# Cross-attention in a decoder layer: where a step's projection tiles stand in TensorE's program

## The chip, the cores and the metric

One core of a Trainium2 chip runs the whole program. The metric is device time in microseconds: the median of three runs. A profile of one execution gives the busy times and the waits.

## The reference

The reference is one decoder layer on x of shape (8, 128, 512), in float32: self-attention with 32 heads, cross-attention with a context of the same shape, a feed-forward part, and a layer norm after each. The change is in the cross-attention, which computes:

```
q = (x @ wq)  -> 32 heads of 128      k, v = (ctx @ wk), (ctx @ wv) -> 8 heads of 128
q, k = rope(q), rope(k)               each k and v head serves 4 query heads
attn = softmax(q @ k.T / sqrt(128) + mask)
out  = (attn @ v, heads side by side) @ wo
```

## The kernel before

**Number format.** Each operand of a product is held as a high and a low half, and each product is made of three matmuls (high by high, low by high, high by low; `product`, line 30). So every copy from PSUM has two parts: ScalarE writes the high half, and VectorE or POOL (GpSimd) the low half, as the difference.

**Steps.** `attend_cross` (line 623) goes over 8 groups g of four query heads that share one k and v head, and in each group over the 8 batch rows s. That makes 64 steps, n = 8g + s, with three more at the end to drain. Groups 1 to 6 are a hardware loop. In step n the core computes the scores of row n, transposes the probabilities of n-2, multiplies them by v, and multiplies the result of n-3 by wo.

**Projections.** While a group is attended, the next one is projected, half of the rows at a time. A half cycle is four steps; u = s % 4 is the place in it. It projects six tiles of 128 by 512, each with 12 matmuls: four query heads (tiles 0 to 3), k (tile 4) and v (tile 5). The places do tiles 0 and 1, tile 2, tiles 3 and 4, tile 5 (`STEPS`, line 631). Even tiles use one PSUM bank, odd ones another. Tiles 0 to 4 are then rotated: three operations on VectorE (`rotate`, line 952), a sum on POOL (line 1060), the high half on ScalarE (line 774), the low half on POOL (line 1065). Tile 5 is copied by ScalarE (line 780) and transposed on TensorE (`turn_values`, line 881).

**Order.** Each engine runs its own program in order, one `step` after another, and semaphores tie them together. The orders are written by hand:

- TensorE (line 888): transposes of the probabilities of n-2 (line 896), scores of n (lines 906, 907), in place 0 the transposes of v, the output product of n-3 with wo (`yb`), the probability-value product of n-2 (`ov`), then the step's projection tiles (`project`, line 863).
- VectorE (line 967): reciprocal, low half of the transposes, mask added to the scores, four maxima, their negation (line 997), in place 0 the low half of v, the output product added to x (line 1007), the low half of `ov` (line 1010), in row 2 the low halves of two pieces of wo (line 1015), then the rotations of this step's tiles.
- ScalarE (line 794): copy of the transposes, high halves of the tiles projected in the step before, four exponentials (line 817), copy of `ov` (line 792), high halves of weight pieces (line 828), in place 3 the copy of tile 5.
- POOL (line 1068): probabilities of n-1 divided by their sums (line 1075), low halves of the tiles of the step before, low halves of weight pieces (line 1088), sums of the rotations of this step.
- SP loads the weight pieces into a ring of five slots, each as the split of the piece before it in that slot ends.

**What a tile waits for.** `project` waits for both halves of its weight piece and for its PSUM bank. For tiles 2 to 5 the bank is free when VectorE has rotated the tile two before (`s_sin`); for tile 0 the rotations of the half cycle before must be done; tile 1 waits for ScalarE's copy of the last tile 5 (`s_vt`). VectorE rotates the tiles of a step as the last work of that step (in the last group, a row's statistics follow).

Of the kernel before, what the change touches and what calls it, by code (L numbers as in the profile page):

```python
# [12 lines left out]
B = 8  # L13
# [16 lines left out]
def product(eng, out, stationary, moving, first, last):  # L30


    for n, (i, j) in enumerate(PASSES):
        mm = eng.matmul(out, stationary[i], moving[j], start=first and n == 0,  # L34
                        stop=last and n == len(PASSES) - 1)
    return mm
# [156 lines left out]
def wait(eng, sem, value):  # L193

    if not isinstance(value, int) or value > 0:
        eng.wait_ge(sem, value)
# [426 lines left out]
def attend_cross(nc, first, wq_d, wk_d, wv_d, wo_d, mask_d, trig_d, ident, xT, cT, w, stage, y, norm, next_norm, weights):  # L623
# [7 lines left out]
    STEPS = {0: (0, 1), 1: (2,), 2: (3, 4), 3: (5,)}  # L631
    K, V, TILES = 4, 5, 6
    PER = 10
    with ExitStack() as ctx:
# [25 lines left out]
        s_chi, s_clo = sem("chi"), sem("clo")  # L660
# [5 lines left out]
        NX = 2 * C  # L666
# [5 lines left out]
        def live(g, s, lag=0):  # L672
            return not isinstance(g, int) or 0 <= B * g + s - lag < NS

        def loop(eng, step):


            for s in range(B):
                step(0, s)
            with eng.Fori(1, G - 1) as g:  # L680
                for s in range(B):
                    step(g, s)
            for g in (G - 1, G):
                for s in range(B):
                    step(g, s)

        def projects(g, s):
            return not isinstance(g, int) or g < G - 1 or (g == G - 1 and s < 4)

        def half_cycle(g, s):  # L690

            return 2 * g + 1 + s // 4
# [7 lines left out]
        def lo_of(g, j):  # L700

            return TILES * g + j + 1
# [22 lines left out]
        @block.sync  # L725
        def _(eng):
            eng.dma_start(trig[:, :, :], trig_d).then_inc(s_const, 16)
            eng.dma_start(mask[:, :, :], mask_d).then_inc(s_const, 16)

            def wait_first(n):  # L730
                kind, j = first.PIECES[n]
                eng.wait_ge(s_wlo if kind == "w" else s_clo, j + 1)

            for n in range(RING, FIRST):
                wait_first(n - RING)
                first.load(eng, n)

            def cycle(g, last=False):
                for j in range(Q if last else PER):
                    what = ("wo", j) if j < Q else ("w", j - Q)  # L740

                    if j < RING and isinstance(g, int) and g == 0:
                        wait_first(FIRST + j - RING)
                    elif j < RING:
                        eng.wait_ge(s_wlo, lo_of(g, j + 1))
                    elif j < PER - 1:
                        h = j - RING
                        eng.wait_ge(s_wolo[h // 2], 2 * g + h % 2 + 1)
                    else:
                        eng.wait_ge(s_wlo, lo_of(g + 1, 0))  # L750
                    src = wo_d[bass.ds(g, 1), :, j, :] if j < Q else \
                        wq_d[bass.ds(g + 1, 1), :, j - Q, :] if j < Q + K else (wk_d if j == Q + K else wv_d)[bass.ds(g + 1, 1)]
                    eng.dma_start(stage[:, slot(what), :], src.rearrange("a p n -> (a p) n")).then_inc(s_piece[slot(what)], 16)

            cycle(0)
            with eng.Fori(1, G - 1) as g:
                cycle(g)
            cycle(G - 1, last=True)
            eng.wait_ge(s_wlo, TILES * G)
            for i in range(2):  # L760
                eng.wait_ge(s_wolo[i], 2 * G)
            for n in range(len(weights.PIECES)):
                weights.load(eng, n)
# [97 lines left out]
        @block.tensor  # L861
        def _(eng):
            def project(H, g, half, j):

                i = TILES * H + j
                eng.wait_ge(s_whi, PER * g + j + 1)
                eng.wait_ge(s_wlo, lo_of(g, j))

                if j == 0:
                    wait(eng, s_sin, 5 * H)  # L870
                elif j == 1:
                    wait(eng, s_vt, H)
                else:
                    eng.wait_ge(s_sin, 5 * H + j - 1)
                cols = slice(half * HALF, (half + 1) * HALF)
                for c in range(C):
                    mm = product(eng, pj[j % 2][:, :], [t[:, j, c * P:(c + 1) * P] for t in w],
                                 [t[:, c, cols] for t in (xT if j < K else cT)], c == 0, c == C - 1)
                mm.then_inc(s_pj, 1)

            def turn_values(H):
                eng.wait_ge(s_vt, H + 1)
                wait(eng, s_vlo, H)
                for t in range(4):
                    mm = eng.transpose(vp[:, t * P:(t + 1) * P], vt[:, t * S:(t + 1) * S], ident)
                mm.then_inc(s_vp, 1)

            def step(g, s):
                n = B * g + s
                H = half_cycle(g, s)  # L890
                u, half = s % 4, 1 - s // 4
                if live(g, s, 2):
                    eng.wait_ge(s_norm, n - 1)
                    wait(eng, s_plo, n - 2)
                    for h in range(Q):
                        mm = eng.transpose(tp[:, h * S:(h + 1) * S], prob[:, s % 2, h * S:(h + 1) * S], ident)  # L896
                    mm.then_inc(s_tp, 1)
                if live(g, s):
                    if u == 0:
                        eng.wait_ge(s_qlo, 5 * H)  # L900
                    wait(eng, s_top, n)
                    tok = slice(s * S, (s + 1) * S)
                    for h in range(Q):
                        out = sc[:, h // 2, h % 2, :, :].rearrange("p j s -> p (j s)")
                        both = k[:, s, :, :].rearrange("p j s -> p (j s)")
                        eng.matmul(out, q[0][:, h, tok], both, start=True, stop=False)  # L906
                        mm = eng.matmul(out[:, 0:S], q[1][:, h, tok], both[:, 0:S], start=False, stop=True)
                    mm.then_inc(s_sc, 1)
                if isinstance(g, int) and g == 0 and s == 0:
                    eng.wait_ge(norm.s_lo, B)  # L910
                    eng.wait_ge(s_clo, NX)
                if u == 0 and live(g, s):
                    turn_values(H - 1)
                if live(g, s, 3):
                    m = n - 3
                    eng.wait_ge(s_ohi, m + 1)
                    eng.wait_ge(s_olo, m + 1)
                    wait(eng, s_add, m)
                    if s == 3:
                        for i in range(2):  # L920
                            eng.wait_ge(s_wolo[i], 2 * (g + 1))
                    for h in range(Q):
                        mm = product(eng, yb[:, :], [t[:, h * S:(h + 1) * S] for t in o],
                                     [t[:, h, :] for t in wo], h == 0, h == Q - 1)
                    mm.then_inc(s_y, 1)
                if live(g, s, 2):
                    m = n - 2
                    eng.wait_ge(s_phi, m + 1)
                    eng.wait_ge(s_plo, m + 1)
                    wait(eng, s_olo, m)  # L930
                    if u == 2:
                        eng.wait_ge(s_vlo, 2 * g + 1 + s // 4)
                    mm = product(eng, ov[:, :], [t[:, (s - 2) % B, :] for t in v], [t[:, :] for t in pT], True, True)
                    mm.then_inc(s_pv, 1)
                if projects(g, s):
                    for j in STEPS[u]:
                        project(H, g + s // 4, half, j)

            for b in range(4):
                norm.transpose(eng, b)  # L940
            eng.wait_ge(norm.s_lo, 4)
            for j in range(TILES):
                if j == K:
                    eng.wait_ge(s_clo, C)
                project(0, 0, 0, j)
            for b in range(4, B):
                norm.transpose(eng, b)
            loop(eng, step)

        @block.vector  # L950
# [556 lines left out]
```

## Time and profile before

| | us |
|---|---|
| median of three runs | 1065.37 (1063.99 to 1065.83) |
| span of the profiled execution | 1065.3 |
| TensorE busy | 987.9 (93%) |
| VectorE busy | 765.2 (72%) |
| ScalarE busy | 503.1 (47%) |
| POOL busy | 437.0 (41%) |

The page gives no time around the span; the span and the median differ by less than 0.1 us. A share of the span is a mean over stages: self-attention comes first, the cross-attention's steps run from about 312 to 926 us, and the feed-forward part ends the program. Busy times of TensorE are modelled from starts, so its work is better read from the distance of one start to the next.

### The profile page before, as it was taken

The numbers are of one execution on the slowest core, as the hardware profiler recorded it, in microseconds if no ns is written. First come the engines' busy times: TensorE is split into PE (matmuls) and PEld (weight loads), VectorE is DVE, ScalarE is ACT, GpSimd is POOL, SyncE is SP. The second block draws the span as 40 slices with busy tenths as digits, with TensorE's granted clock in tenths as the row PEclk, the third lists the DMA queues.
The fourth block names the chain that finished last, engine by engine and source line by source line (L and its number), as shares of the span: only waits on it lengthen the run. The fifth ranks groups of instructions, "written<-read, shape, count | busy, mean of one in ns | idle before, by whom it ended". The sixth has DMA issues, their size and how long they took to land. (4 is left out here: it accounts for less than half of the span.)

```text
span 1065.3 us, 17470 instructions
## 1 busy us (share of the span) xinstructions
PE 987.9 (93%) x4940; PEld 825.1 (77%) x4940; DVE 765.2 (72%) x2345; ACT 503.1 (47%) x1581; POOL 437.0 (41%) x367
## 2 busy tenths in 40 slices
PE   6997999999778999999999999999999999789996
PEld 5875999999556887887887887787778777578885
DVE  4445568888697787777877877777777788784646
ACT  4325669898335435445345435444444435441220
POOL 1762000000357556546546646637546455340101
PEclk9997579999899999999999999999999999999998
DMA  8032212222221102002002002002001002210001
GB/s 298 1 99 60 60 37 59 46 58 70 87 82 50 40 11 65 31 5 69 30 0 76 22 0 79 20 0 79 20 15 64 10 18 73 78 62 10 30 1 39
DMA packets 41372, 52.02 MB, mean 49 GB/s; under 512 B 5104, under 2 KB 21616, under 8 KB 41200
## 3 DMA queue, kind: packets, MB, share of 16 engines
q1 hardware_dynamic: 41008, 50.44, 15.6%
q0 software_dynamic: 320, 1.05, 0.3%
q8 instruction: 21, 0.34, 0.1%
q14 instruction: 23, 0.19, 0.1%
HBM read 40.98 MB, written 2.10 MB: 40 GB/s over the span
## 5 line engine op out<-in xcount | busy, mean ns | idle before, releaser
L1060 POOL TENSOR_TENSOR C_t<-C_t 128x512 f32<-128x512 f32 x80 | 104.5, 1310 | 153.2 <-DVE C_t L965 153.2
L817 ACT ACTIVATE C_prob<-C_prob,C_ntop 128x128 f32<-128x128 f32 x256 | 99.8, 391 | 87.9 <-DVE C_ntop L997 87.8
L34 PE MATMUL C_yb<-C_woh,C_oh 128*128 128x512 f32 x256 | 107.5, 420 | 17.4 <-POOL C_wol L1088 12.3
L774 ACT ACTIVATE C_qh<-C_t 128x512 fp32r<-128x512 f32 x64 | 40.5, 633 | 141.0 <-POOL C_t L1060 141.0
L1010 DVE TENSOR_TENSOR C_ol<-C_ov,C_oh 128x512 fp32r<-128x512 f32 x64 | 44.2, 691 | 85.8 <-ACT C_oh L792 85.8
L34 PE MATMUL C_pj<-xTh,wh 128*128 128x512 f32 x256 | 101.3, 396 | 3.7 <-DVE xTl L128 2.2
L492 ACT ACTIVATE B_prob<-B_prob,B_ntop 128x128 f32<-128x128 f32 x256 | 99.2, 392 | 8.5 <-DVE B_ntop L573 7.3
L34 PE MATMUL C_yb<-C_woh,C_ol 128*128 128x512 f32 x256 | 102.8, 402 | 0.0
L34 PE MATMUL C_yb<-C_wol,C_oh 128*128 128x512 f32 x256 | 102.6, 401 | 0.0
L34 PE MATMUL C_pj<-xTh,wl 128*128 128x512 f32 x256 | 100.8, 394 | 0.0
L34 PE MATMUL C_pj<-xTl,wh 128*128 128x512 f32 x256 | 100.6, 393 | 0.0
L1065 POOL TENSOR_TENSOR C_ql<-C_t,C_qh 128x512 fp32r<-128x512 f32 x64 | 82.3, 1297 | 3.0 <-ACT C_qh L774 3.0
L961 DVE TENSOR_TENSOR C_t<-C_pj,C_trig 128x512 f32<-128x512 f32 x80 | 55.0, 687 | 32.7 <-PE C_pj L34 30.9
L1088 POOL TENSOR_TENSOR wl<-stage,wh 128x512 fp32r<-128x512 f32 x42 | 53.8, 1288 | 55.8 <-ACT wh L828 55.8
L34 PE MATMUL B_sc<-kd,qs 128*128 128x512 f32 x192 | 69.8, 479 | 5.7 <-PEq L226 3.1
L801 ACT ACTIVATE C_pTh<-C_tp 128x512 fp32r<-128x512 f32 x64 | 37.5, 586 | 76.0 <-PE C_tp L896 76.0
L1075 POOL TENSOR_TENSOR C_prob<-C_prob,C_rden 128x512 f32<-128x512 f32 x64 | 66.7, 1042 | 15.7 <-DVE C_rden L974 15.7
L34 PEld LDWEIGHTS C_yb<-C_woh,C_oh 128*128 128x128 f32 x256 | 49.5, 193 | 29.6 <-issue 17.7
L906 PE MATMUL C_sc<-C_k,C_qh 128*128 128x256 f32 x256 | 67.8, 342 | 2.1 <-POOL C_k L1065 2.1
L527 PE MATMUL B_ov<-vhl,B_pTl 128*128 (+1 forms) x256 | 66.0, 278 | 0.0
L596 DVE TENSOR_TENSOR B_pTl<-B_tp,B_pTh 128x512 fp32r<-128x512 f32 x64 | 44.1, 689 | 30.2 <-ACT B_pTh L485 30.2
L101 POOL TENSOR_TENSOR first_norm_rstd<-first_norm_moments,power 128x4 f32<-128x4 f32 x2 | 2.1, 1032 | 148.8 <-DVE first_norm_moments L88 148.8
(219 smaller groups left out, 2867.1 us busy)
## 6 DMA issues: line engine op xcount, KB each, us to landing
stage<-wq_dram SPq DMA_DIRECT2D x32, 256.0 KB, 3.4
stage<-wo_dram SPq DMA_DIRECT2D x32, 256.0 KB, 3.1
qs<-q SPq DMA_DIRECT2D x16, 256.0 KB, 2.7
kd<-k SPq DMA_DIRECT2D x128, 32.0 KB, 2.0
stage<-wqkvT_dram SPq DMA_DIRECT2D x10, 256.0 KB, 5.9
x<-x_nat_dram SPq DMA_DIRECT2D x1, 2048.0 KB, 10.1
stage<-wk_dram SPq DMA_DIRECT2D x8, 256.0 KB, 3.2
stage<-ctxT_dram SPq DMA_DIRECT2D x8, 256.0 KB, 3.0
```

The source lines that it names most:

```text
L34: mm = eng.matmul(out, stationary[i], moving[j], start=first and n == 0, stop=last and n == len(PASSES) - 1)
L492: last = eng.activation(e, e, ACT.Exp, bias=ntop[:, G % 4, h:h + 1], scale=1.0, accum_out=total[:, HG * G + h:HG * G + h + 1])
L527: mm = eng.matmul(out[:, at:at + DH], pT[1][:, G % 2, h * S:(h + 1) * S], v[:, 0:DH], start=False, stop=True)
L596: eng.tensor_tensor(pT[1][:, G % 2, :], tp[G % 2][:, :], pT[0][:, G % 2, :].bitcast(F32), ALU.subtract).then_inc(s_plo, 1)
L817: last = eng.activation(e, e, ACT.Exp, bias=ntop[:, s % 2, h:h + 1], scale=1.0, accum_out=total[:, s % 2, h:h + 1])
L906: eng.matmul(out, q[0][:, h, tok], both, start=True, stop=False)
L961: eng.tensor_tensor(split(t1[:, j % 2, :]), split(bank[:, :]), cos, ALU.mult).then_inc(s_cos, 1)
L1010: eng.tensor_tensor(o[1][:, :], ov[:, :], o[0][:, :].bitcast(F32), ALU.subtract).then_inc(s_olo, 1)
L1060: eng.tensor_tensor(t1[:, j % 2, :], t1[:, j % 2, :], t2[:, j % 2, :], ALU.add).then_inc(s_sum, 1)
L1065: eng.tensor_tensor(lo, t1[:, j % 2, :].rearrange("p (b s) -> p b s", s=S), hi.bitcast(F32), ALU.subtract).then_inc(s_qlo, 1)
L1075: eng.tensor_tensor(e, e, rden[:, (s - 1) % 2, :].unsqueeze(2).broadcast_to([P, Q, S]), ALU.mult).then_inc(s_norm, 1)
L1088: eng.tensor_tensor(lo, stage[:, slot(what), :], hi.bitcast(F32), ALU.subtract).then_inc(s_wolo[1] if kind == "wo" else s_wlo, 1)
```

## The change

In TensorE's `step`, the projection tiles move from the end of the step to its start, ahead of the transposes. The two waits of step 0 for the transposed x and the context move with them. Nothing else changes: no other engine's program, no semaphore, no buffer.

```
@@ def step(g, s), TensorE
                 u, half = s % 4, 1 - s // 4
+                if isinstance(g, int) and g == 0 and s == 0:
+                    eng.wait_ge(norm.s_lo, B)
+                    eng.wait_ge(s_clo, NX)
+                if projects(g, s):
+                    for j in STEPS[u]:
+                        project(H, g + s // 4, half, j)
                 if live(g, s, 2):
                     eng.wait_ge(s_norm, n - 1)
...
                     mm.then_inc(s_sc, 1)
-                if isinstance(g, int) and g == 0 and s == 0:
-                    eng.wait_ge(norm.s_lo, B)
-                    eng.wait_ge(s_clo, NX)
                 if u == 0 and live(g, s):
                     turn_values(H - 1)
...
                     mm.then_inc(s_pv, 1)
-                if projects(g, s):
-                    for j in STEPS[u]:
-                        project(H, g + s // 4, half, j)
```

## Rows read from the trace of the kernel before

**Rows 1.** Windows of the cross-attention: bounds, length, busy us (count) per engine, PEclk, DMA.
```profile
311.67:344.66 32.99, 28.51 (x138) 23.45 (x138) 25.51 (x77) 16.07 (x50) 19.48 (x16) 0.95 0.13 40
344.66:882.92 538.26, 519.60 (x2577) 430.36 (x2577) 413.77 (x1134) 242.19 (x725) 304.28 (x251) 0.99 0.10 34
```

**Rows 2.** Timeline, TensorE, steps 0 and 29: start us, us, operation, idle before and releaser.
```profile
313.01 0.66 PE L885 MATMUL C_vp<-ident,C_t 128*128 128x128 f32 x4 [0.21 <-DVE xTl L128]
313.43 0.48 PE L34 MATMUL C_pj<-xTh,wh 128*128 128x512 f32 x1
...
585.93 0.60 PE L896 MATMUL C_tp<-ident,C_prob 128*128 128x128 f32 x4
...
587.24 0.45 PE L34 MATMUL C_yb<-C_woh,C_oh 128*128 128x512 f32 x1
```

**Rows 3.** Timeline, TensorE, the rest of step 29 and the start of 30.
```profile
590.05 0.39 PE L34 MATMUL C_ov<-C_pTh,C_vh 128*128 128x512 f32 x1
...
590.74 0.39 PE L34 MATMUL C_pj<-xTh,wh 128*128 128x512 f32 x1
...
593.46 0.60 PE L896 MATMUL C_tp<-ident,C_prob 128*128 128x128 f32 x4
```

**Rows 4.** Waits, TensorE, 282 to 890: us in total, times, longest.
```profile
PE C_yb L34 <- POOL C_wol L1088: 12.3, 8, 1.8
...
PE C_pj L34 <- DVE C_t L965: 4.9, 3, 2.0
```

**Rows 5.** Timeline, ScalarE, step 29 and the start of 30.
```profile
586.57 0.60 ACT L801 ACTIVATE C_pTh<-C_tp 128x512 fp32r<-128x512 f32 x1 [4.34 <-PE C_tp L896]
587.08 0.64 ACT L774 ACTIVATE C_qh<-C_t 128x512 fp32r<-128x512 f32 x1
...
592.08 0.40 ACT L817 ACTIVATE C_prob<-C_prob,C_ntop 128x128 f32<-128x128 f32 x1 [1.65 <-DVE C_ntop L997]
...
593.64 0.58 ACT L792 ACTIVATE C_oh<-C_ov 128x512 fp32r<-128x512 f32 x1
594.12 0.62 ACT L828 ACTIVATE wh<-stage 128x512 fp32r<-128x512 f32 x1
```

**Rows 6.** Timeline, VectorE, steps 28 and 30.
```profile
579.37 0.17 DVE L997 TENSOR_SCALAR C_ntop<-C_top 128x4 f32<-128x4 f32 x1
...
597.09 0.66 DVE L977 TENSOR_TENSOR C_pTl<-C_tp,C_pTh 128x512 fp32r<-128x512 f32 x1
...
599.41 1.26 DVE L997 TENSOR_SCALAR C_ntop<-C_top 128x4 f32<-128x4 f32 x1
...
602.88 0.69 DVE L1010 TENSOR_TENSOR C_ol<-C_ov,C_oh 128x512 fp32r<-128x512 f32 x1 [1.61 <-ACT C_oh L792]
603.48 0.68 DVE L961 TENSOR_TENSOR C_t<-C_pj,C_trig 128x512 f32<-128x512 f32 x1
...
605.62 0.69 DVE L961 TENSOR_TENSOR C_t<-C_pj,C_trig 128x512 f32<-128x512 f32 x1
```

**Rows 7.** Timeline ahead of the loop: end of a rotation on VectorE, start on TensorE.
```profile
293.07 0.68 DVE L965 TENSOR_TENSOR C_t<-C_pj,C_trig 64x512 f32<-64x512 f32 x1
293.90 0.47 PE L34 MATMUL C_pj<-xTh,wh 128*128 128x512 f32 x1 [1.45 <-DVE C_t L965]
```

**Rows 8.** Timeline, POOL, step 30.
```profile
599.36 1.29 POOL L1065 TENSOR_TENSOR C_ql<-C_t,C_qh 128x512 fp32r<-128x512 f32 x1
```

**Rows 9.** Timeline, VectorE, step 2: its two splits of wo.
```profile
333.68 1.28 DVE L1015 TENSOR_TENSOR C_wol<-stage,C_woh 128x512 fp32r<-128x512 f32 x2
```

**Rows 10.** Timeline, TensorE, one stall ahead of step 2's probability-value product.
```profile
328.09 0.76 PE L34 MATMUL C_ov<-C_pTh,C_vh 128*128 128x512 f32 x1 [2.76 <-issue]
```

**Rows 11.** Windows after two stalls and around a third, with the granted clock.
```profile
328.09:331.21 3.12, 3.12 (x7) 2.45 (x8) 2.71 (x12) 0.93 (x2) 2.76 (x3) 0.50 0.00 0
...
412.40:418.00 5.60, 3.87 (x17) 3.25 (x18) 5.44 (x17) 1.24 (x3) 5.60 (x6) 1.00 0.79 231
...
491.80:495.17 3.37, 3.37 (x9) 2.60 (x8) 3.26 (x15) 1.26 (x2) 3.37 (x4) 0.50 0.54 181
```

## The prediction

> **What bounds the kernel now.** I read the page first, then the stretches, then the waits of TensorE, then one step on each engine. The chain that ended last covers only the tail of the program and says nothing of the cross-attention, so the stretch table decides. From the score products of step 4 to those of step 60 it shows 538.26 us, with TensorE busy 519.60 of them at clock 0.99; VectorE comes next with 413.77 [rows 1]. That stretch is 14 half cycles of four steps, 38.45 us each. TensorE's own work in one half cycle, from starts to next starts [rows 2, 3]: six projection tiles of 2.72 (590.74 to 593.46), four times transposes and scores 1.31 (585.93 to 587.24), output product 2.81 (to 590.05) and probability-value product 0.69 (to 590.74), one value transpose 0.42 (313.01 to 313.43): 16.3 + 19.2 + 0.4 = 36.0. So 2.5 us of a half cycle are lost now. The one wait that recurs is the output product on POOL's split of wo, 12.3 us in 8 waits; projection tiles wait for a rotation on VectorE three times only, 4.9 us, and all three lie ahead of the loop [rows 4]. The tiles at a step's end are what keeps TensorE busy while ScalarE and VectorE finish that step.
>
> **What the change does.** Per tile it moves 12 matmuls, their 12 weight loads and their semaphore waits, from behind the probability-value product to ahead of the transposes. No instruction is added or removed and no DMA belongs to a tile. Nothing moves on SP, POOL, ScalarE or VectorE; the two waits moved in step 0 are for work that ends where the trace starts the value transposes. SP's weight loads hang on splits that wait for a tile's end, which comes no later within a step than now; at no cost.
>
> The cost is in what a tile waits for. Tile 2 (place 1) needs the rotation of tile 0, tile 4 (place 2) that of tile 2, tile 5 (place 3) that of tile 3: each time a rotation that VectorE issues as the last thing of the step before, behind its max, its add of the output product and its split of the probability-value product. Today a tile comes a step's worth of TensorE work after that; then it stands first. Queued behind the waiting tile on TensorE are the transposes and scores of that very step, from which ScalarE and VectorE live, so nobody can work ahead.
>
> **The path in one step.** From the first transpose to the next tile: copy of the transposes starts after 0.64 and takes 0.60 [rows 2, 5]; VectorE's low half, mask add and four maxima take 2.32 up to the negation [rows 6]; negation 0.17; four exponentials 1.56; copy of the probability-value product 0.58 [rows 5]; its split 0.60, the rotation's three operations 2.11 (2.14 to the next rotation's start) [rows 6]; TensorE starts 0.15 after a rotation ends (293.07 + 0.68 to 293.90) [rows 7]. With three or four hand-overs at 0.03 to 0.04 that is 8.87.
>
> The negation took 0.17 or 1.26. The long one begins at 599.41 and ends at 600.67, with POOL's split that ran from 599.36 to 600.65 [rows 6, 8]: it waits out the POOL operation. In place 1 POOL then splits two tiles behind the copies, starting 1.8, 3.05 after the transposes (0.64, 0.51 to the next ScalarE start, 0.64 [rows 5], then 1.29 each [rows 8]); the negation is due at 3.6, inside the second, which ends at 4.3. I take 0.55 there; bounds 0 and 1.1. In place 2 only one such split is left and it is over by 3.1.
>
> **The sum of a half cycle.**
> - Place 0: two tiles, 5.44; transposes and scores 1.31, values 0.42, output 2.81, probability-value 0.69, its drain 0.16 (0.39 long, 0.23 apart); then copy, split, rotation and hand-overs 3.50: 14.33. TensorE is idle 3.5 of it.
> - Place 1: 2.72 + 8.87 + 0.55 = 12.1. TensorE reaches tile 3 after 7.53 (2.72 + 1.31 + 2.81 + 0.69) and is through it after 10.25: idle about 1.8 before tile 4.
> - Place 2: 2.72 + 8.87 = 11.6, TensorE idle 3.9. Once in two half cycles VectorE also splits two pieces of wo here: 1.28 [rows 9].
> - Place 3: 7.53; the next two tiles need nothing that is late. Only in the half cycles with wo the second of them waits for ScalarE's two weight copies (0.52 each [rows 5]) and its value copy ahead: 0.8.
>
> Together 45.6, and for two half cycles 91.2 + 1.3 + 0.8 = 93.3 against 76.9 now (538.26 / 7): 8.2 more per half cycle, with the 1.7 us wait on wo gone (POOL has a step longer for it) and counted in the 76.9. Over 14: 115. The first half cycle now takes 32.99 [rows 1]; by the same path, with the products that its first steps lack left out, tile 0 starts near 313.0 [rows 2], tile 2 comes 11.2 after it, tile 4 8.3 later, tile 5 12.9 (8.87, 2.72 and wo's 1.28), the next tile 0 8.3 (7.53 and 0.8) and the scores of step 4 another 5.8: 359.5, where they stand at 344.66, 14.8 later. At step 60 there are no tiles to go ahead of the scores, so 5.4 comes off. Sum at full clock: 115 + 14.8 - 5.4 = 124.
>
> **The clock.** After the idle 2.76 us at 328.09 TensorE ran at half rate, 0.50 granted (1.2 of 2.4 GHz), seven matmuls in 3.12 us, 0.43 apart where 0.23 is usual; that is 1.4 lost, and 1.6 with an eighth [rows 10, 11]. Of the eight waits on wo, seven last about 1.7 us; three of the seven were followed by such a spell (491.80 to 495.17) and four not (412.40 to 418.00 stayed at 1.00) [rows 4, 10, 11]. So each of the two long stalls of a half cycle, 3.5 and 3.9, will bring one; as part of the spell can fall into the stall itself I take 1.2 of a possible 1.6 (bounds 0 and 1.6): 15 x 2 x 1.2 = 36. The 1.8 before tile 4 brings one three times in seven: 15 x 0.43 x 1.2 = 8. The tile that runs slow stands on the path, so this adds in full: 44.
>
> The Trainium skill, TensorE: Matmul & The Clock Gate, section "HAM oscillation — how this bites in real kernels", warns of just such a gap that returns in every turn of a loop, but sets the harm at gaps longer than those of 1.7 to 2.8 us after which the rows here show the fall; the trace disagrees on that point. [...]
>
> Forecast: 1065.3 + 124 + 44 = 1233. The span of the profiled execution, 1065.3, is within 0.1 of the median of the runs, 1065.37, so the sum stands against either.
>
> **Rivals.**
> 1. The stalls come but the clock stays, except after the longest (3.9 + 1.3, once a cycle): 1065.3 + 124 + 7 x 1.2 = 1198. For it: four of seven gaps of 1.7 left the clock at 1.00. Against: 2.76 did not. Chance 0.16. [...]
> 2. Only the stall at tile 2 bites, because VectorE, whose chain now runs beside the tiles, gets ahead by places 2 and 3: 36.0 + 3.7 + 0.8 a half cycle, 2.0 more than now, 30 in 15, and a spell of slow clock each, 18: 1114. For it: VectorE has 124 us of slack over the stretch. Against: it stands in order behind this step's scores. Chance 0.10.
> 3. The other side: TensorE gets faster. The wait on wo (1.7 in each of seven cycles) and its three slow spells go, 12 + 5, and tiles run on without waiting: 1048. It decides at tile 2: if VectorE's rotation of tile 0 is done when TensorE leaves place 0. It would have to be issued ahead of the split that needs the probability-value product, and in VectorE's program it is behind it. Chance 0.03; that no more than noise comes of all this, 0.02.
> 4. Everything is paid in full: 1.6 per spell, 1.1 at the negation, tile 4 slow each time: 124 + 15 x 0.55 + 15 x 3 x 1.6 = 204, 1270. Chance 0.07.
>
> **Numbers.** The forecast's own case has 0.62. Range 1188 to 1258: from no clock loss at all (1065 + 124) to most of the fourth case. About 0.2 is left outside, most of it below. A change under 0.2% (2 us) can't be told from none. Faster 0.03, same 0.02, slower 0.95.
>
> **What would show it.** In the profile after: TensorE idle ahead of the projection tiles for the rotation (its last line on VectorE), some 45 waits, 9 to 10 us per half cycle, and 130 to 150 in all where there are 4.9 now; the wait on POOL's split of wo gone or nearly; the eight steps of a cycle some 99 us apart instead of 77; TensorE's clock of the stretch at 0.90 to 0.94. ScalarE's and VectorE's busy times stay as they are, apart from the negation's. It would be wrong if a tile's wait ended on something else (the low half of a weight piece, for which POOL stands), if the transposes' wait on POOL's normalisation came last, or if a cycle came out under 90 us.

## The result and the profile after

The changed kernel takes 1248.42 us (median of four runs, 1245.05 to 1250.24) where the kernel before takes 1064.68 beside it (1062.39 to 1065.83). The ratio is 1.1739, with an interval of [1.1683, 1.1796]. The forecast was 1233, its range 1188 to 1258. The profiled execution has a span of 1247.5 us, 182.2 more than before.

First the stretches of the program after: bounds, length, busy time and count of PE, PEld, DVE, ACT and POOL, granted clock, DMA share, GB/s. The bounds are the score products of steps 0, 4 and 60 and the end.

```profile
318.59:364.87 46.28, 32.20 (x140) 25.68 (x138) 23.72 (x75) 16.28 (x50) 23.01 (x19) 0.82 0.11 38
364.87:1062.50 697.63, 558.49 (x2556) 452.20 (x2553) 395.29 (x1132) 237.37 (x719) 301.46 (x248) 0.91 0.08 26
1062.50:1247.50 185.00, 162.34 (x749) 131.78 (x747) 116.87 (x263) 58.73 (x137) 42.96 (x40) 0.95 0.11 38
```

Against [rows 1], the 14 half cycles from step 4 to step 60 take 159.4 us more (697.63 against 538.26). The scores of step 4 come 20.2 later (364.87 against 344.66), and from step 60 to the end it is 2.6 more (185.00 against 1065.30 - 882.92 = 182.38). TensorE's clock in the long stretch fell from 0.99 to 0.91, and it stood idle for 139 us of it (697.63 - 558.49) where it was 19.

The waits of TensorE from 300 to 1090 (us in all, times, longest) say for what:

```profile
PE C_pj L34 <- DVE C_t L965: 148.9, 46, 7.1
PE C_pj L34 <- POOL wl L1088: 5.7, 7, 0.8
```

The rotation on VectorE (line 965), three waits in [rows 4], now stops TensorE 46 times, 45 of them in the half cycles (the first, 2.0 us long, lies ahead of step 0, as before). The wait of the output product on wo is gone. One half cycle on TensorE's timeline, the first matmul of the tile after each stall (start, duration, operation, idle before and releaser); the first row is the same tile 5 in the half cycle before, where VectorE also splits wo:

```profile
549.48 0.79 PE L34 MATMUL C_pj<-cTh,wh 128*128 128x512 f32 x1 [5.01 <-DVE C_t L965]
...
574.90 0.51 PE L34 MATMUL C_pj<-xTh,wh 128*128 128x512 f32 x1 [3.43 <-DVE C_t L965]
...
588.73 0.50 PE L34 MATMUL C_pj<-cTh,wh 128*128 128x512 f32 x1 [1.70 <-DVE C_t L965]
...
600.34 0.79 PE L34 MATMUL C_pj<-cTh,wh 128*128 128x512 f32 x1 [3.82 <-DVE C_t L965]
```

Tile 2 waits 3.43, tile 4 1.70, tile 5 3.82 or 5.01: three stalls in each of the 15 half cycles. What the clock does behind them stands in windows that begin where these stalls end, that of tile 2 with its second matmul (columns as above):

```profile
549.48:556.09 6.61, 6.61 (x25) 5.34 (x25) 2.27 (x5) 0.68 (x2) 4.99 (x5) 0.60 0.47 154
575.24:578.62 3.38, 3.38 (x9) 2.61 (x8) 1.88 (x4) 0.00 (x0) 2.52 (x3) 0.50 0.22 70
588.73:593.00 4.27, 4.27 (x25) 3.72 (x26) 0.30 (x2) 0.77 (x2) 2.29 (x2) 1.00 0.19 61
```

Tile 5 starts at half rate (1.2 of 2.4 GHz), tile 2 too in this half cycle, tile 4 runs at full rate.

### The profile page after: what moved, and what is told of

Read it like the earlier page. It is cut to its first block and busy times, and to the rows that moved or that the text cites. A ratio compares the mean times of both kernels' runs of the same rounds, so it can differ in the third digit from the quotient of the medians.

```text
span 1247.5 us, 17458 instructions
## 1 busy us (share of the span) xinstructions
PE 1040.7 (83%) x4940; PEld 857.0 (69%) x4940; DVE 746.4 (60%) x2345; ACT 499.8 (40%) x1581; POOL 438.0 (35%) x367
## 3 DMA queue, kind: packets, MB, share of 16 engines
q0 software_dynamic: 320, 1.05, 0.3%
## 5 line engine op out<-in xcount | busy, mean ns | idle before, releaser
L977 DVE TENSOR_TENSOR C_pTl<-C_tp,C_pTh 128x512 fp32r<-128x512 f32 x64 | 44.1, 690 | 230.5 <-ACT C_pTh L801 230.5
L34 PE MATMUL C_pj<-xTh,wh 128*128 128x512 f32 x256 | 110.2, 430 | 64.2 <-DVE C_t L965 54.4
L34 PE MATMUL C_pj<-cTh,wh 128*128 128x512 f32 x128 | 67.9, 531 | 97.5 <-DVE C_t L965 97.5
L817 ACT ACTIVATE C_prob<-C_prob,C_ntop 128x128 f32<-128x128 f32 x256 | 99.8, 391 | 117.9 <-DVE C_ntop L997 117.8
L34 PEld LDWEIGHTS C_pj<-cTh,wh 128*128 128x128 f32 x128 | 32.2, 252 | 117.3 <-DVE C_t L965 83.2
L34 PEld LDWEIGHTS C_pj<-xTh,wh 128*128 128x128 f32 x256 | 53.1, 207 | 84.9 <-DVE C_t L965 46.6
L34 PE MATMUL C_pj<-xTh,wl 128*128 128x512 f32 x256 | 108.6, 424 | 0.0
L34 PE MATMUL C_pj<-xTl,wh 128*128 128x512 f32 x256 | 107.6, 420 | 0.0
L34 PE MATMUL C_pj<-cTl,wh 128*128 128x512 f32 x128 | 63.9, 499 | 0.0
```

Of the source, the lines that this page charges most:

```text
L817: last = eng.activation(e, e, ACT.Exp, bias=ntop[:, s % 2, h:h + 1], scale=1.0, accum_out=total[:, s % 2, h:h + 1])
L977: eng.tensor_tensor(pT[1][:, :], tp[:, :], pT[0][:, :].bitcast(F32), ALU.subtract).then_inc(s_plo, 1)
```

## The experiments

Each ratio is to the kernel before, on the same chip. "Excess" is the median less that kernel's own median there; the change's own is 183.7.

**1. A third PSUM bank for the tiles.** The bank of the value transposes joins the ring, so that a tile waits for a rotation one tile older.

```
+        def bank_of(H, j):
+            return pj[j % 2] if isinstance(H, int) and H == 0 else (*pj, vp)[j % 3]
...
+                elif j == 2:
+                    eng.wait_ge(s_vlo, H)
                 else:
-                    eng.wait_ge(s_sin, 5 * H + j - 1)
+                    eng.wait_ge(s_sin, 5 * H + j - 2)
```

> Tiles first as in the change, but over three PSUM banks (the value bank vp takes tiles 2 and 5), so that a tile waits for a rotation one step older. Theory W (the time is the wait of tiles 2, 4 and 5 for a rotation that VectorE issues last in the step before): the 152 us of waits on rotations fall below 10, the clock returns to 0.98 or more, and what is left is the wait on POOL's split of wo in row 3, longer than the 1.7 us of before since one tile instead of two lies ahead of it, some 4.4 us a cycle: 1070 to 1100 us. Rival O (the order itself: transposes and scores behind the tiles starve ScalarE and VectorE, the bank has no part in it): stays above 1220 us.

Measured: 1141.28 (1139.72 to 1142.84), ratio 1.0760 [1.0692, 1.0828], excess 81. TensorE's waits, 300 to 1000:

```profile
PE C_pj L34 <- POOL wl L1095: 24.2, 13, 3.2
PE C_yb L34 <- POOL C_wol L1095: 22.3, 8, 3.3
PE C_vp L34 <- POOL wl L1095: 18.0, 6, 3.0
...
PE C_pj L34 <- DVE C_t L972: 1.9, 1, 1.9
```

The rotation is gone from the list but for one wait, and with it 102 us of the excess: the dependency, not the order as such, makes the stalls. The time expected was missed on the high side, and the clock of the stretch comes back to 0.95 only, not to 0.98. In place of the rotation the low halves of weight pieces come last: of the k and v pieces (the first and the third row) and of wo. POOL splits them as late in a step as VectorE rotates.

**2. Something to do in the stall.** Ahead of tiles 2, 4 and 5 TensorE runs matmuls into the idle bank, whose results nobody reads.

```
+                        if j == 2:
+                            eng.wait_ge(s_vlo, H)
+                        for i in range({2: 13, 4: 5, 5: 14}.get(j, 0)):
+                            eng.matmul(vp[:, :], xT[0][:, 0, 0:P], xT[0][:, 0, 0:HALF], start=True, stop=True)
```

> The change, with matmuls that only fill TensorE's idle time (13 ahead of tile 2, 5 ahead of tile 4, 14 ahead of tile 5, into the value bank, which nothing reads then). The waits for rotations stay, the idle time in which the clock falls does not. Theory W with the clock as a second cost: no half-rate spell in the steps, 3.5 us a half cycle less, 1196 us, within 1185 to 1210. Rival C (the half-rate spells lie in time that TensorE would wait anyway): no change, 1240 to 1255 us. If the fillers themselves delay the tiles: above 1255.

Measured: 1205.04 (1202.28 to 1207.95), ratio 1.1353 [1.1278, 1.1427]. Its stretch of 14 half cycles and its wait for the rotation:

```profile
364.65:1023.62 658.97, 620.56 (x3003) 507.51 (x3002) 395.53 (x1132) 237.57 (x719) 302.24 (x248) 0.99 0.08 27
```

```profile
PE C_pj L34 <- DVE C_t L969: 36.4, 43, 3.9
```

The granted clock is back at 0.99 and 39 us are gone, of the excess (183.7 to 145) as of the stretch (697.63 to 658.97), though every tile still starts when its rotation allows. So the slow matmuls sat on the path. Half cycles without wo take 45.7 us (the first 45.9), which is the prediction's sum at full clock (45.6). Those with wo take 48.4 to 49.8, not 47.7: their last stall outlasts the 14 matmuls, and behind it slow spells remain in most of them. So the clock's whole share is over 39.

**3. Tile 2 alone at the front** (in the kernel before; all other tiles stay last).

```
+                if projects(g, s):
+                    for j in STEPS[u]:
+                        if j in (2,):
+                            project(H, g + s // 4, half, j)
...
-                        project(H, g + s // 4, half, j)
+                        if j not in (2,):
+                            project(H, g + s // 4, half, j)
```

> The kernel before with tile 2 alone moved to the front of its step; the other tiles stay last. Theory W: tiles 0 and 1 then run right ahead of tile 2, VectorE rotates tile 0 while tile 1 runs (2.7 us against a rotation of 2.1), so tile 2 waits under 0.5 us; 1062 to 1085 us. Rival S (each tile moved pays its own stall, so the costs of the moves add up): 3.5 us of waiting and a half-rate spell in each of 15 half cycles, 1065 + 15 x 4.8 = 1137 us.

Measured: 1075.20 (1074.38 to 1079.15), ratio 1.0143 [1.0077, 1.0209], excess 15. Waits, 300 to 900:

```profile
PE C_yb L34 <- ACT C_oh L792: 18.6, 14, 1.4
PE C_yb L34 <- POOL C_wol L1093: 12.2, 7, 1.8
```

No tile waits for a rotation. Where tiles 0 and 1 still end place 0, they give VectorE the time to rotate tile 0; the 3.4 us stall comes only when these tiles have moved as well. What a tile costs at the front depends on where the tile before it stands, so the costs of the single moves don't add up to that of the change. The small loss has a cause that was not expected: place 1 now ends without a tile, and the next step's output product reaches ScalarE's copy of the probability-value product too soon.

**4. Rotations earlier on VectorE** (right after the negation, ahead of the two operations that need TensorE's late products).

```
+                if projects(g, s):
+                    for j in STEPS[u]:
+                        if j < V:
+                            rotate(H, j)
                 if u == 0 and live(g, s):
...
```

> The change, with VectorE's rotations moved too: right behind the negation of the maxima, ahead of the add of the output product and the split of the probability-value product, into the time in which VectorE waits for the exponentials. Theory W: a rotation ends about 6 us after the step's transposes, tile 4 no longer waits, tiles 2 and 5 wait about 1 us: 38 to 40 us a half cycle, 1055 to 1095 us. Rival V (the split of the probability-value product, now behind the rotations, comes late for the output product, so the wait only changes place): output products wait 2 us or more in each step, 1150 us or more.

Measured: 1136.99 (1133.95 to 1140.35), ratio 1.0715 [1.0643, 1.0786], excess 77. Waits, 300 to 1000:

```profile
PE C_pj L34 <- DVE C_t L965: 31.2, 23, 4.3
PE C_pj L34 <- POOL wl L1088: 31.0, 17, 3.0
PE C_yb L34 <- DVE C_wol L1019: 14.9, 7, 2.3
```

Four fifths of the rotation waits go (31.2 of 148.9 us are left), without another bank and with TensorE's program as it was: what stops the tile is where the rotation stands in VectorE's own order. The expected time was missed for the reason of experiment 1: the weight pieces come next.

**5. The third bank in the kernel before**, as a control (the edit of experiment 1).

> Control: the kernel before (tiles last) with the three PSUM banks of e1. Theory W: no tile in the loop waited for a rotation before, so the third bank changes nothing: within 0.5% of the kernel before. Rival B (the bank by itself makes the tiles flow faster, and e1 owes its gain to that and not to the wait taken away): faster than before by 1% or more.

Measured: 1062.14 against 1062.03, ratio 0.9985 [0.9957, 1.0013]. The bank alone is worth nothing, so what experiment 1 won back is stalls.

**6. The third bank, and the k and v pieces split a step earlier.**

```
-                   4: [("w", 3)], 5: [("w", K)], 6: [("w", V)]}
+                   4: [("w", 3), ("w", K)], 5: [("w", V)]}
```

> e1 (tiles first, three banks), with the splits of the k and v weight pieces issued one step earlier on ScalarE and POOL. In e1 tiles 4 and 5 waited 3.1 and 3.0 us a cycle for POOL's split of those pieces, which was issued in the step right before. Theory W (a tile in front waits for whatever the step before issues last, and each such wait costs itself and a half-rate spell): both waits go, 7 x (6.1 + 2 to 3) = 57 to 64 us less than e1, 1075 to 1090 us; the wait on wo of 2.7 us a cycle stays. Rival O (tiles in front cost by their order, since the scores come later): above 1120 us.

Measured: 1102.42 (1099.23 to 1109.92), ratio 1.0394 [1.0338, 1.0449], excess 40. Waits, 300 to 1000:

```profile
PE C_yb L34 <- POOL C_wol L1095: 22.3, 8, 3.4
PE C_pj L34 <- ACT C_t L783: 13.3, 7, 1.9
PE C_ov L34 <- issue: 11.2, 9, 2.0
PE C_pj L34 <- POOL wl L1095: 5.2, 7, 0.9
```

The two rows of weight pieces (42.2 us) shrink to 5.2, and half of the excess goes with them. Next in the list are wo and ScalarE's copy of tile 5 (line 783), for which tile 1 waits.

**7. As 6, with tile 4 back at the end of its step**, to give POOL time for wo.

```
-                        project(H, g + s // 4, half, j)
+                        if j != K:
+                            project(H, g + s // 4, half, j)
...
+                if projects(g, s) and u == 2:
+                    project(H, g + s // 4, half, K)
```

> e8 with tile 4 back at the end of its step, the other tiles first. Two tiles then lie again between the probability-value product of row 2 and the output product of row 3 that waits for wo. Theory W: the wait on wo falls from 2.7 to under 1 us and its half-rate spell with it, 10 to 25 us less than e8: 1055 to 1075 us. Rival: tile 4 in the rear leaves ScalarE and VectorE later, and e9 is slower than e8.

Measured: 1106.33 (1103.16 to 1108.96), ratio 1.0401 [1.0356, 1.0445], excess 44. Waits, 300 to 1000:

```profile
PE C_yb L34 <- POOL C_wol L1098: 13.8, 8, 1.8
...
PE C_yb L34 <- issue: 10.0, 15, 0.7
PE C_pj L34 <- POOL wl L1098: 8.1, 7, 2.3
```

A miss: the time is within the spread of 6. The wait on wo falls by 8.5 us as expected, and short waits elsewhere take most of it back; where the rest stays was not followed up.

**8. As 6, with the split of wo swapped**: POOL takes the pieces 0 and 1, VectorE 2 and 3, which the product needs last.

```
-                    if what in (("wo", 0), ("wo", 1)):
+                    if what in (("wo", 2), ("wo", 3)):
```

> e8 with the four splits of wo dealt the other way: POOL takes the first two pieces, VectorE (0.6 us each against POOL's 1.3) the last two. The last low half is then ready about 1.1 us earlier. Theory W: the wait on wo goes from 2.7 to about 1.6 us a cycle, and some of its half-rate spells go too: 8 to 18 us less than e8. Rival: VectorE, which now waits longer for ScalarE's copies ahead of its rotations, gives it back: no change.

Measured: 1134.15 (1131.90 to 1139.89), ratio 1.0686 [1.0636, 1.0737], excess 72: 32 more than 6, where less was expected. Waits, 300 to 1000:

```profile
PE C_pj L34 <- POOL wl L1095: 22.5, 7, 3.2
PE C_yb L34 <- DVE C_wol L1022: 20.9, 8, 3.2
```

The wait on wo stays nearly as long and only changes its engine. The first row has grown from 5.2; these waits are for tile 1's weight piece. One cycle shows where it comes from, VectorE's splits of wo and then ScalarE's copies of the weight pieces in the step behind:

```profile
419.93 2.51 DVE L1022 TENSOR_TENSOR C_wol<-stage,C_woh 128x512 fp32r<-128x512 f32 x2 [0.87 <-ACT C_woh L831]
```

```profile
432.37 1.14 ACT L831 ACTIVATE wh<-stage 128x512 fp32r<-128x512 f32 x2
```

VectorE's two splits, now beside POOL's, take 2.51 where they take 1.28 in 6. Its rotations start behind them, its next negation comes later, and so do ScalarE's exponentials and the copies behind them: the copies start 9.8 us after the output product (422.59), where it is 6.7 in 6 (419.42 to 426.10). The load of the piece is not the reason. It was issued at 420.39 and landed at 423.56, and ScalarE came to the copies without idle time.

**9. As 6, without two needless waits.** Tile 0 waits for the rotation that its bank needs instead of all five, and tile 1 no longer for the copy of tile 5, which has another bank now.

```
-                if j == 0:
+                if isinstance(H, int) and H < 2 and j < 2:
...
-                elif j == 1:
...
+                elif j < 2:
+                    eng.wait_ge(s_sin, 5 * H - 1 + j)
```

> e8 without two waits that three banks make needless: tile 1 no longer waits for ScalarE's copy of tile 5 (1.9 us a cycle in e8), tile 0 no longer for the rotation of tile 4. Theory W: that wait and its share of half-rate spells go, 7 x 2.2 = 15 us less than e8: 1080 to 1092 us. Rival D (TensorE now runs ahead of VectorE's chain, which sets the pace: mask, maxima, exponentials, copy, split, rotations): the time goes into the probability-value product's wait for the transposes' low half, no change against e8, 1097 or more.

Measured: 1087.73 (1084.17 to 1092.60), ratio 1.0236 [1.0173, 1.0299], excess 26. Stretch from step 4 to step 60, and waits, 300 to 1000:

```profile
353.22:902.15 548.93, 514.15 (x2555) 428.98 (x2554) 412.72 (x1132) 245.50 (x722) 300.10 (x248) 0.98 0.10 33
```

```profile
PE C_yb L34 <- POOL C_wol L1096: 22.3, 8, 3.3
PE C_ov L34 <- issue: 11.2, 9, 2.0
```

From one score start to that four steps on, half cycles without wo take 37.4 to 37.5 us, where the kernel before has 37.0 to 37.3. So the new order itself costs next to nothing once no tile waits. Those with wo take 41.5 to 43.0 against 39.4 to 40.4 (the last one of each set aside, as no tile follows it): most of what is left sits there. Each wait on wo is 2.8 us on average (22.3 / 8), where it was 1.5 in [rows 4].

**10 and 11. As 9, with ScalarE's wo copies ahead of its exponentials**, and then with the early rotations of experiment 4 as well.

```
+                for what in splits(g, s):
+                    if what[0] == "wo":
+                        split(what)
...
```

> e14 with ScalarE's copies of the four pieces of wo ahead of the exponentials of row 2, not behind them. Theory W: POOL gets them some 2 us earlier, the wait on wo falls from 2.7 to under 1 us: 15 to 25 us less than e14, 1055 to 1075 us. Rival D: the exponentials come 2 us later, VectorE's chain with them, and the gain is lost: no change against e14.

> e15 with VectorE's rotations right behind the negation, as in e5. With tiles in front their rotations can start before the exponentials are done, so VectorE no longer waits 1.6 us a step for ScalarE's copy. If VectorE's chain sets the pace in e14 and e15 (rival D there): TensorE's own 36 us a half cycle come into reach, 37 to 38 a half cycle, 1035 to 1060 us, at or below the kernel before. If TensorE's waits are all that counts (W alone): no faster than e15, since the split of the probability-value product comes later.

Measured: 1109.45 (1105.32 to 1112.83), ratio 1.0432 [1.0370, 1.0494], and 1093.72 (1084.46 to 1098.96), ratio 1.0262 [1.0181, 1.0342]. Both missed. Waits, 300 to 1000, of the first

```profile
PE C_yb L34 <- DVE C_wol L1030: 20.9, 8, 3.2
PE C_pj L34 <- POOL wl L1103: 19.4, 6, 3.3
```

and of the second:

```profile
PE C_yb L34 <- DVE C_wol L1034: 31.2, 8, 5.4
PE C_yb L34 <- DVE C_ol L1029: 14.4, 22, 1.5
```

Earlier copies don't make wo earlier: the pieces now wait for VectorE, which splits two of them behind the step's other work, and behind the rotations in the second kernel.

**12. The kernel before, with the fourth piece of wo split on VectorE instead of POOL**, against the wait of [rows 4] (POOL's own test and the counts of the semaphores follow).

```
-                    if what in (("wo", 0), ("wo", 1)):
+                    if what in (("wo", 0), ("wo", 1), ("wo", 3)):
```

> The kernel before (tiles last, two banks), with the low half of wo's fourth piece on VectorE instead of POOL, so that POOL splits one piece and VectorE three. It aims at the one wait that recurs in the kernel before and that e14 shows as all that is left of the price of tiles in front. The last low half is then ready about 2.9 us behind ScalarE's copy of the probability-value product instead of 4.2. Theory W: the wait of 1.7 us falls under 0.5 us and the half-rate spells behind it go, 7 x (1.3 + 0.7) = 14 us less: 1045 to 1055 us, faster than both kernels. Rival D: VectorE's rotations of that step come 0.9 us later and the wait moves to the next output product: within 0.4% of the kernel before.

Measured: 1075.54 (1072.89 to 1083.72), ratio 1.0132 [1.0099, 1.0164]: slower. Waits, 300 to 1000, then the split on VectorE and POOL's work beside it:

```profile
PE C_ov L34 <- issue: 21.3, 17, 2.8
PE C_vp L888 <- ACT C_t L783: 7.1, 11, 1.3
PE C_yb L34 <- DVE C_wol L1018: 6.9, 7, 1.1
```

```profile
412.05 1.49 DVE L1018 TENSOR_TENSOR C_wol<-stage,C_woh 128x512 fp32r<-128x512 f32 x1 [0.20 <-ACT C_woh L831]
413.46 0.68 DVE L964 TENSOR_TENSOR C_t<-C_pj,C_trig 128x512 f32<-128x512 f32 x1
```

```profile
411.58 1.41 POOL L1091 TENSOR_TENSOR C_wol<-stage,C_woh 128x512 fp32r<-128x512 f32 x1 [3.84 <-ACT C_woh L831]
412.95 1.73 POOL L1091 TENSOR_TENSOR wl<-stage,wh 128x512 fp32r<-128x512 f32 x1
```

The wait on wo shrinks, from 1.5 a time to 1.0, and the program still loses 15 us. The added split took 1.49 where the two of [rows 9] took 1.28 together, and the rotations start behind it. TensorE's loss shows ahead of the probability-value product, as "issue", a row that names no releaser. The low half of the transposes in the next step, and that product:

```profile
417.83 0.66 DVE L980 TENSOR_TENSOR C_pTl<-C_tp,C_pTh 128x512 fp32r<-128x512 f32 x1
```

```profile
418.59 0.47 PE L34 MATMUL C_ov<-C_pTh,C_vh 128*128 128x512 f32 x1 [2.00 <-issue]
```

The low half ends at 418.49 and the product starts 0.10 later, as behind all 17 of these waits. So TensorE waits for VectorE, which is late by the added split: the expected time was missed and the rival seen beforehand is nearer, though with the wait at another product and more lost than it had.

No version was faster than the kernel before.

## Why the prediction was right

**The mechanism.** It said that a tile at the front waits for a rotation which VectorE issues last in the step before. The 46 waits on line 965 show it; experiments 1 and 4 remove most of it from either end, by the bank and by VectorE's order, and the time follows. Experiment 5 excludes that the bank helps by itself. Rival 2, in which only tile 2 stalls, and rival 3, faster, fell: all three stalls recur in each half cycle. Rival 4, everything paid in full (1270), had the price of a spell at tile 5 nearer, and at tile 4 took one in each half cycle where none came.

**The path in one step.** From the first transpose to the next tile 8.87 was worked out, and 9.42 with the slow negation in place 1. From the transposes at 591.59 to tile 5 at 600.34 it is 8.75, from those at 579.36 to tile 4 at 588.73 it is 9.37. The stalls, forecast as 3.5, 1.8, 3.9 and 5.2 (with wo), are 3.43, 1.70, 3.82 and 5.01. The negation in place 1, VectorE first, then POOL:

```profile
530.87 0.78 DVE L997 TENSOR_SCALAR C_ntop<-C_top 128x4 f32<-128x4 f32 x1
```

```profile
529.08 2.55 POOL L1065 TENSOR_TENSOR C_ql<-C_t,C_qh 128x512 fp32r<-128x512 f32 x2 [1.78 <-ACT C_qh L774]
```

0.78 is 0.61 more than the 0.17 that it takes alone, where 0.55 was taken; it ends at 531.65 with POOL's second split (531.63).

**The sum at full clock.** 124 us were forecast. Experiment 2 meets its half cycle without wo to 0.1 us (45.7 against 45.6).

**The wait on wo** was to go, and is gone. The cycles of eight steps were to be 99 us; six of the seven take 99.8 to 101.7, and the last, at whose end no tiles stand, 93.3. The clock was to be 0.90 to 0.94 and is 0.91.

**Where the 15 us lie that were missing** (14 of them in the profiled spans: 182.2 against 168). The term that was mis-sized is the clock's, at each of three places. By the prediction 14 half cycles were to add 110 at full clock (115 - 5.4) and 41 of slow clock, 151; they add 159.4, 8.8 more. Half of TensorE's busy time at a granted clock of 0.50 is what the clock costs, and summed over the records of the trace that is 50.8 us there, not 41. Less this cost the half cycles take 45.4 to 45.5 without wo and 47.8 to 48.0 with it, where the sum has 45.6 and 47.7. The parts of a half cycle, by the matmuls that start 0.43 apart instead of 0.23 behind each stall:
- Tile 5: all 15 stalls (3.79 to 5.09, the first 7.05) have a spell, of 8 to 12 matmuls, some 10.7 on average, 2.1 us (10.7 x 0.20). The prediction took 1.2 and bounded it at 1.6, from the one spell of seven or eight that it had seen.
- Tile 2: the first stall, of 4.28, has one of 11; of the 14 others (3.43 to 3.53) 10 have one, of 6 to 8 matmuls, 1.05 a half cycle on average, near the 1.2 taken.
- Tile 4: none in 15 stalls of 1.33 to 1.78, where three in seven were taken from the waits on wo of the same length [rows 10, 11], 0.5 a half cycle.

So 3.2 in place of 2.9 is seen in spells, and 3.6 in the lengths of the half cycles (50.2 against 46.65 at full clock); the other 0.4 lies in transposes and scores, where a spell outlasts its tile. That tile 4 had none offset half of what tile 5 cost too much; this much of the near hit is luck.

The first half cycle lost 2.5 more than forecast (20.2 against 14.8 and its share of the clock, 2.9): by the same count the clock cost 5.5 there, behind stalls of 4.28 and 7.05. The stretch behind step 60 lost 2.6 where nothing was expected: the clock cost 6.0 there, and 3.3 in the kernel before. Why it fell for longer in that stretch, which the change leaves as it was, is open.

Rival 1, the clock that stays, fell: experiment 2 is nearly the kernel that it describes, and it is 39 us faster than the changed one. The Trainium skill, TensorE: Matmul & The Clock Gate, section "HAM oscillation — how this bites in real kernels", puts the harm on the longer gaps alone, and by its bound the stalls at tiles 2 and 5 are long enough and those at tile 4 are not. In this trace that ordering holds better than the prediction granted, with no spell behind 1.3 to 1.8 us, one in 10 of 14 behind 3.4 to 3.5 and one behind each stall of 3.8 and more; the spells behind 1.7 in the kernel before [rows 11] stay against it.

**What the prediction had seen as a danger.** It named the low half of a weight piece as a wait that could come in between. In the changed kernel that wait comes seven times, 0.8 us each (5.7 in all), at tile 1 in the half cycles with wo, where the sum had 0.8 for ScalarE's copies of the pieces. It is the first thing behind the rotation, though, and the expectations of experiments 1 and 4 overlooked it.

## What to carry to other kernels

In programs that run in order, a piece of work is not only filler for the engine that does it: at the end of a step it buys the other engines the time for their last operation, and at the front it waits for exactly that operation. Before moving it, look up which operation frees its buffer and at which place in its own engine's step that stands; then count as many stalls as there are such pairs, with what the clock takes behind each. Removing the first wait shows the next one (rotation, weight pieces, copy of v, wo): four edits took 158 of 184 us back and still left the kernel slower than the one before.

## What the runs showed of the hardware that was not expected

- **Half-rate spells differ with the stall.** Behind 3.79 to 7.05 us of idle TensorE ran 8 to 12 matmuls at half rate, behind 3.43 to 3.53 us 6 to 8 or, four times in 14, none, behind 1.33 to 1.78 us none in 15 at one place of the program, and behind 1.7 us three spells in seven at another. What decides between 8 and 12, and between the two places, is open.
- **VectorE's small operations wait out POOL's.** The 128x4 negation takes 0.17 us alone, 0.78 here, 1.26 before [rows 6], each long one ending with a POOL operation. In the kernel before 45 of 64 are long, most of them 1.25, after the change 29, of 0.78; all 64 take 54.0 us before and 28.6 after, which is more than the 19 us by which VectorE's busy time fell (765.2 to 746.4). Experiment 12 shows the same of a split with two inputs in SBUF: 1.49 us, where the splits of [rows 9] take 0.64 each, where it began beside POOL's split, which ended at 412.99, and POOL's next took 1.73 instead of 1.28. The Trainium skill, SBUF — State Buffer, section "Who interferes with whom", says that VectorE shares a port pair with GpSimd for the second of two inputs in SBUF and in its two-port modes, which a tensor_scalar can take, and that whichever of the two issues first holds the pair for its whole instruction while the other blocks. The numbers of the split agree with it: 412.99 and a split of 0.64 make 413.6, and VectorE's ended at 413.54.
- **The "issue" rows ahead of the probability-value product** (11.2 us in experiments 6 and 9, 21.3 in 12) name no releaser. In each of these 35 waits the product starts 0.10 us after VectorE has ended the low half of the transposes, so by the times that is what TensorE waits for.
